# Graph network with LSTM windows on one core: first loads split over two queues, constants awaited later, and the rounding of the recurrent weights moved from VectorE to ScalarE

## What is computed

```
h = relu(adj @ (x @ Wg0 + bg0))
h = relu(adj @ (h @ Wg1 + bg1))
for p in 1..4:                       # windows of p nodes, last hidden state written back
    last = lstm_last(Wih[p-1], Whh[p-1], bih[p-1], bhh[p-1], windows(h, p))
    h[:, idx] = last
x = layernorm(x + h)
agg = A_hat @ x                      # adj + I, scaled by 1/sqrt(degree) on both sides
out = batchnorm(relu(batchnorm(agg @ W1.T + b1)) @ W2.T + b2)
x = layernorm(x + out)
```

## Time and profile before

| | |
|---|---|
| median of 3 runs | 818.66 us (818.16 to 818.75) |
| the profiled execution | 818.31 us, its span 816.5 us |
| PE busy | 782.5 us (96%), 4952 matmuls |
| DVE busy | 719.1 us (88%) |
| ACT busy | 591.8 us (72%) |
| POOL busy | 73.7 us (9%) |
| chain that ended last | PE 79%, DVE 10%, ACT 6% |
| mean granted TensorE clock | 0.992 |

### The profile page before, as it was taken

One profiled execution on the slowest core, in us unless ns is written; L12 is line 12 of the kernel. 1 busy time (PEld: TensorE's weight loads), 2 busy tenths in 40 slices (PEclk: granted clock), 3 DMA queues, 4 the chain that ended last, 5 costly groups with the idle time before them and its releaser, 6 DMA issues.

```text
span 816.5 us, 15519 instructions
## 1 busy us (share of the span) xinstructions
PE 782.5 (96%) x4952; PEld 535.3 (66%) x4952; DVE 719.1 (88%) x1819; ACT 591.8 (72%) x1178; POOL 73.7 (9%) x76
## 2 busy tenths in 40 slices
PE   8999999999999999999999999999999977899985
PEld 5666777777767776777677767776765754344542
DVE  4787989999999999999999999999999986588897
ACT  4666777777777777777777777777777853794398
POOL 0000000000000000000000000000000000000696
PEclk9999999999999999999999999999999999999998
DMA  6010001010101010101010101010000101144245
GB/s 198 26 50 3 1 27 53 34 45 27 52 28 52 26 51 26 51 26 51 26 51 26 51 26 51 27 53 27 26 26 27 53 27 51 53 153 155 77 177 210
DMA packets 17693, 44.97 MB, mean 55 GB/s; under 512 B 2032, under 2 KB 3184, under 8 KB 17520
## 3 DMA queue, kind: packets, MB, share of 16 engines
q1 hardware_dynamic: 17648, 44.39, 15.4%
HBM read 27.61 MB, written 16.78 MB: 54 GB/s over the span
## 4 chain that ended last, share of the span: by engine, by line
PE 79%; DVE 10%; ACT 6%; issue 2%; POOL 1%; DMA 1%; SPq 1%; ACTq 0%; DVEq 0%; POOLq 0%
PE gate_bank L902 14%; PE gate_bank L903 14%; PE gate_bank L939 7%; PE gate_bank L917 6%; PE gate_bank L927 6%; PE back_bank L856 3%; PE front_bank L821 3%; PE front_bank L810 3%; ACT z L1050 3%; PE front_bank L827 3%; PE front_bank L815 3%; PE gate_bank L886 3%; PE gate_bank L887 2%; PE gate_bank L888 2%; PE gate_bank L910 2%
## 5 line engine op out<-in xcount | busy, mean ns | idle before, releaser
L902 PE MATMUL gate_bank<-h_hi,w_hi 128*128 128x256 f16 (+2 forms) x528 | 161.9, 307 | 4.4 <-DVE h_lo L1263 2.9
L903 PE MATMUL gate_bank<-h_hi,w_lo 128*128 128x256 f16 (+2 forms) x528 | 161.7, 306 | 0.0
L1000 ACT ACTIVATE gate_i<-gate_bank,lstm_bias 128x512 f32<-128x512 f32 (+2 forms) x176 | 99.5, 566 | 62.3 <-PE gate_bank L927 32.1
L1000 ACT ACTIVATE gate_o<-gate_bank,lstm_bias 128x512 f32<-128x512 f32 (+2 forms) x176 | 100.0, 568 | 30.4 <-PE gate_bank L927 20.0
L917 PE MATMUL gate_bank<-h_lo,w_hi 128*128 128x256 f16 (+2 forms) x384 | 115.8, 301 | 0.0
L902 PE MATMUL gate_bank<-s_hi,w_hi 128*128 128x256 f16 (+2 forms) x384 | 112.7, 302 | 1.3 <-DVE s_hi L1260 1.3
L903 PE MATMUL gate_bank<-s_hi,w_lo 128*128 128x256 f16 (+2 forms) x384 | 112.6, 302 | 0.0
L1246 DVE SCALAR_TENSOR_TENSOR gate_f<-gate_o,gate_f 128x512 f32<-128x512 f32 (+2 forms) x176 | 94.8, 539 | 19.1 <-ACT gate_f L1006 18.1
L1006 ACT ACTIVATE gate_f<-cell 128x512 f32<-128x512 f32 (+2 forms) x176 | 89.7, 510 | 29.1 <-DVE cell L1243 14.8
L1000 ACT ACTIVATE gate_g<-gate_bank,lstm_bias 128x512 f32<-128x512 f32 (+2 forms) x176 | 99.5, 565 | 0.6
L927 PE MATMUL gate_bank<-s_lo,w_hi 128*128 128x256 f16 (+2 forms) x384 | 99.2, 302 | 0.0
(11 more groups left out here) (195 smaller groups left out, 1665.3 us busy)
## 6 DMA issues: line engine op xcount, KB each, us to landing
x_front<-in_x SPq DMA_DIRECT2D x16, 512.0 KB, 4.1
rows_sb<-in_x SPq DMA_DIRECT2D x16, 512.0 KB, 3.3
x_kept<-normed_sb SPq DMA_DIRECT2D x16, 512.0 KB, 2.6
z<-x_kept SPq DMA_DIRECT2D x16, 512.0 KB, 3.7
out<-z SPq DMA_DIRECT2D x15, 512.0 KB, 3.1
z<-in_wr SPq DMA_DIRECT2D x1, 1536.0 KB, 7.1
out<-z SPq DMA_DIRECT2D x2, 256.0 KB, 2.6
z<-in_wih SPq DMA_DIRECT2D x1, 192.0 KB, 2.6
```

The lines of the kernel that those rows point to most:

```text
L902: mm(dst, w[0], v[0], start=start, stop=False)
L903: mm(dst, w[1], v[0], start=False, stop=False)
L1000: ins = activation(acts[gate][h][:, 0:n], gate_bank[h][bank_of(job, gate)][:, 0:n], ACT.Tanh if gate == "g" else ACT.Sigmoid, bias=lstm_bi ...
```

## The change

Six things are done.

1. adjT_sb is no longer loaded by SP but by ACT, as its first instruction. SP loads x_front of half-step (0, 0) in two parts of 256 KB, and PE waits for the first part in front of mix0's first bank and for the second in front of the second bank.
2. ACT runs a sigmoid of one column first, so that its table load of the sigmoid set comes at the start.
3. DVE's wait for the eight constants, the sum of the LSTM biases and the scaled identity move from in front of lin0's biases to behind them, into split_input_weights.
4. The rounding of slice 0 of w_hi is done by ACT, behind mix1's second output of half-step (0, 0), where ACT now waits for w_stage.
5. The rounding of slices 1 and 2 and of gw1_hi is done by ACT, behind the second relu of lin0 of half-step (0, 1).
6. DVE keeps the subtractions at their old places and waits there for ACT's semaphore weights_high.

```diff
@@ -629,8 +631,8 @@
-            sp.dma_start(adjT_sb[:], adjT).then_inc(sem_adjT, 16)
-            sp.dma_start(flat(x_front[:]), x[0]).then_inc(sem_x, 16)
+            sp.dma_start(x_front[:, 0, :], x[0][:, 0:BANK]).then_inc(sem_x_first, 16)
+            sp.dma_start(x_front[:, 1, :], x[0][:, BANK:2 * BANK]).then_inc(sem_x, 16)
@@ -801,7 +803,10 @@
                 if stage == "mix0":
-                    if (n, i) == (0, 0):
+                    if isinstance(g, int) and (g, h) == (0, 0):
+                        if i == 0:
+                            pe.wait_ge(sem_x if n else sem_x_first, 16)
+                    elif (n, i) == (0, 0):
                         pe.wait_ge(sem_x, loads(g, h))
@@ -982,8 +987,31 @@
             activation = nc.scalar.activation
+            act.dma_start(adjT_sb[:], adjT).then_inc(sem_adjT, 16)
+
+            act.wait_ge(sem_zeros, 1)
+            activation(small[:, 0:1], s_hi[0][:, 0:1], ACT.Sigmoid)
+
+            def weights_high(s):
+                activation(w_hi[:, s], w_stage[:, s], ACT.Copy, scale=W_SCALE).then_inc(sem_high, 1)
+
+            def first_weights():
+                act.wait_ge(sem_wr, 16)
+                weights_high(0)
+
+            def other_weights():
+                weights_high(1)
+                weights_high(2)
+                activation(gw1_hi[:], gw1_stage, ACT.Copy, scale=W_SCALE).then_inc(sem_high, 1)
+
+            first_pair = {(0, ("mix1", "out", 1)): first_weights, (1, ("lin0", "out", 1)): other_weights}
...
@@ -1091,10 +1119,6 @@
             ve.tensor_copy(bias0[:], setup_bank[:, 0:P]).then_inc(sem_degree, 1)
-            dve.wait_ge(sem_loaded, 16 * LOADS)
-            ve.tensor_tensor(lstm_bias[:], lstm_bias[:], bhh_sb[:], ALU.add).then_inc(sem_setup, 1)
-            dve.wait_ge(sem_setup_pool, 1)
-            ve.tensor_scalar(normed_sb[:, 1, P:2 * P], ident[:], small[:, 3:4], None, ALU.mult).then_inc(sem_setup, 1)
             dve.wait_ge(sem_degree, 5)
@@ -1103,16 +1127,19 @@
             def split_input_weights():
 
+                dve.wait_ge(sem_loaded, 16 * LOADS)
                 ve.tensor_copy(wih1_hi[:], wih1_stage).then_inc(sem_wih, 1)
                 dve.wait_ge(sem_wih, 1)
                 ve.tensor_tensor(wih1_lo[:], wih1_stage, wih1_hi[:].bitcast(F32), ALU.subtract).then_inc(sem_wih, 1)
+                ve.tensor_tensor(lstm_bias[:], lstm_bias[:], bhh_sb[:], ALU.add).then_inc(sem_setup, 1)
+                dve.wait_ge(sem_setup_pool, 1)
+                ve.tensor_scalar(normed_sb[:, 1, P:2 * P], ident[:], small[:, 3:4], None, ALU.mult).then_inc(sem_setup, 1)
 
             def split_weights(s):
 
                 if s == 0:
                     dve.wait_ge(sem_wr, 16)
-                ve.tensor_scalar(w_hi[:, s], w_stage[:, s], W_SCALE, None, ALU.mult).then_inc(sem_degree, 1)
-                dve.wait_ge(sem_degree, 6 + s)
+                dve.wait_ge(sem_high, s + 1)
@@ -1120,8 +1147,7 @@
             def prepare_back():
 
-                ve.tensor_scalar(gw1_hi[:], gw1_stage, W_SCALE, None, ALU.mult).then_inc(sem_degree, 1)
-                dve.wait_ge(sem_degree, 9)
+                dve.wait_ge(sem_high, 4)
```

More of the change, by code:

```diff
@@ L518, in gnn_lstm_kernel @@
         sem_x = sem("x_front_loaded")
+        sem_x_first = sem("x_first_loaded")
+        sem_high = sem("weights_high")
         sem_xb = sem("x_back_loaded")
```

4 lines of the change are left out of this document (added).

## The result

The changed kernel took 814.58 us (median of 5 executions, 814.04 to 815.33), the kernel before 818.2 us beside it (5 executions, 816.94 to 818.75): a ratio of 0.9962 with an interval of 0.9948 to 0.9976. A second measurement with more executions gave 815.38 us (9, from 813.87 to 816.74) against 818.33 us (21, from 815.36 to 820.24), a ratio of 0.9968, 0.9957 to 0.9979. The medians lie 3.6 and 3.0 us apart; the ratios make it 3.1 and 2.6 us, and by the intervals anything from 1.7 to 4.3 us.

What follows compares the result with a forecast made beforehand. PE was taken to bound the loop, and VectorE to be what others wait for between 40 and 50 us. Gains of 0.84 + 0.72 + 0.31 = 1.87 us off 818.66 gave 816.8 us, range 815.2 to 818.2.

Steps and rivals of the forecast that it cites:

- The start: Before 16.97 us: gates about 1.4 us earlier, counted as 0 because PE waits for the second x_front; bounds 0 and 1.4.
- Place one: Around 18 to 23 us: VectorE loses a rounding, hidden state up to 0.5 us earlier, 0.12 carried on.
- Place two: 24 to 30 us: VectorE loses a 0.72 us rounding; with 0.12 carried on, PE starts 0.84 us earlier.
- ScalarE's block: Three roundings on ScalarE before h_hi, 24 to 30 us: 2.55 us, costing 0 up to 2.77 us, 0.4 at 3.15.
- Place three: 40 to 48 us: VectorE drops a rounding before `mixed`, gain 0.72 us; bounds 0.3 and 0.72.
- Place four: 50 to 53 us: gw1's rounding leaves VectorE, `h_lo` comes earlier, gain 0.31 us; bounds 0.1 and 0.4.
- The sum: Whole kernel: 0.84 + 0.72 + 0.31 = 1.87 us gained, profiled execution 818.31 to 816.44 us; chance 0.60.
- The clock at the end: Last half-step and tail: no term in the sum; nothing more was to come after 50 to 53 us.
- The median shown: Whole kernel: median 0.35 us above the profiled execution, so 818.66 - 1.87 = 816.8 us.
- More than summed: Rival at the start: second x_front lands earlier or isn't PE's stop, so 1.4 us count too: 815.4 us; chance 0.08.
- Slower, by the clock: Rival: PE's clock falls in its idle time before 16.97 us, 3.3 us lost, 1.87 won: 820.1 us; chance 0.04.

Runs made afterwards that it cites:

- the start alone: Changed kernel with all roundings back on VectorE, keeping its loads, early table load and late constants: 816.63 us, ratio 0.9987.
- the roundings alone: Changed kernel with the old loads, constants' wait, bias sum and scaled identity, keeping roundings and early table load on ScalarE: 814.82 us, ratio 0.9967.
- 28 zero matmuls: 28 instead of 20 matmuls on zeros before the last half-step's and the tail's products: kernel before 815.92 us, changed kernel 813.54 us.
- a variant: Changed kernel with the rounding of slice 2 back on VectorE: 816.13 us, ratio 0.9979.
- the one execution of 1158.64 us: Sixth execution of the changed kernel with 28 instead of 20 matmuls on zeros, mean granted clock 0.653; that run's median was 813.54 us.

## Why the prediction came out too high

- **The start, counted as nothing: right within the landing's scatter, for this order of loads.** It brought lin1 forward by 1.69 us and PE's work on the second x_front by 0.15; averaged over seven profiles with it and four without, by 0.13. The change without its start runs as fast (ratio 0.9967 against 0.9968), and moving that one load forward by one place brings 1.1 us. The reason given, a landing 0.09 us ahead of PE's start, was enough to see it.
- **Place one, 0.12 carried on: too small.** From x_front to the bias at lin0 (22.98 before, 22.56 after) it is 6.01 us before and 5.74 after, so 0.27 was carried; 0.15 more came with the landing. The step that failed here is "its products release the biases from 22.98 on". In the kernel before, lin0's product ran from 21.66 and VectorE was the late one, busy without a gap up to the bias:

```profile
21.66 1.02 PE L815 MATMUL front_bank<-mixed,w_sb 128*128 128x512 f32 x2
...
22.38 0.68 DVE L1237 TENSOR_TENSOR cell<-gate_i,gate_g 128x512 f32<-128x512 f32 x1
```

  The product was there by 22.68 and the bias began at 22.98, 0.60 us behind the start of the cell. With a rounding less, VectorE is ready sooner, and the bias follows the product at once (21.50 + 1.02 = 22.52, bias at 22.56). From x_front to place two it was 12.48 us before, 12.24 with the start alone, 11.40 with the roundings alone (0.72 of the 1.08 is the rounding at place two) and 11.50 with both: either part gives the carry (0.24 and 0.36), and both together give it once (0.26).
- **Place two, 0.84: 1.13 measured.** The rounding is worth 0.72 as summed, 28.32 - 27.58 = 0.74 from `mixed` to PE is as before, and the 0.29 over it are the two items of place one.
- **ScalarE's block: right.** Estimated 1.07 for 128x1024, 0.41 for gw1 and 2.55 for the block; the rows have 1.06, 0.40 and 2.34 (24.77 to 27.11, since two roundings in a row overlap and take 1.99). The reader at 28.18 found h_hi written.
- **Place three, 0.72: 0.90 measured** (18.24 us from place two before, 17.34 after). The rounding itself is worth 0.74: that is the run with it given back (18.08) against the change. The other 0.16 is a step that I had not in the sum. From the split at 43.91 to the bias at 44.41 it is 0.50 us before, and 42.06 to 42.40 = 0.34 after. The product that this bias reads is no part of it, since it began at 41.81 and was done 1.6 us ahead. Before, from VectorE's and PE's timelines:

```profile
43.91 0.43 DVE L1260 CAST h_hi<-gate_f 128x512 f16<-128x512 f32 x1
44.41 0.69 DVE L1160 TENSOR_TENSOR h0T<-back_bank,bias 128x512 f32<-128x512 f32 x1
...
41.81 1.02 PE L815 MATMUL back_bank<-mixed,w_sb 128*128 128x512 f32 x2
```

  and in the run with the rounding of slice 2 back on VectorE:

```profile
44.58 0.43 DVE L1289 CAST h_hi<-gate_f 128x512 f16<-128x512 f32 x1
44.93 0.68 DVE L1189 TENSOR_TENSOR h0T<-back_bank,bias 128x512 f32<-128x512 f32 x1
```

  The step is 0.35 there and 0.50 in the run with the start alone. So it goes with the other roundings that left VectorE and not with the one of place three; why it shrinks is open.
- **Place four, 0.31: 0.32 measured.**
- **The sum: 1.87 forecast, 2.35 to 2.4 in the trace.** The first rstd averages 98.02 us over three profiles (the kernel before twice, and with 28 zero matmuls) and 95.54 over the same three of the changed kernel: 2.5 us. Of these, 0.3 are landings (PE's start on the second x_front averages 16.90 and 16.61), and 2.2 lie behind it.
- **The clock at the end: put at nothing, and this is the largest miss.** The sum takes 1.87 us off the profiled execution (818.31) and then off "The median shown", 0.35 above it, as if all the rest of the time stood still. For the clock, the prediction says "no row of this trace shows it". The trace of the kernel before does show it: PE idles for 2.54 us in front of 686.28, and the products behind took 1.77 + 1.92 us, with a granted clock of 0.50 from 687 us on. In that profile the two stretches at the end have their long forms (13.59 and 61.44 us), which other executions of the same kernel have shorter, by 1.3 and 1.7 us, and the range had no term for it.
- **The miss added up.** The profiled execution of the changed kernel is also its median, 814.58 us, 2.2 below the 816.8 forecast: 0.5 from the places that were sized too small and the landing, 1.3 from the clock at the last half-step, and 0.35 from the step from the profiled execution to the median. The first is the change's but for the landing; the other two are luck of the draw. That the clock's places also shift the medians is argued from the profiles and the granted clocks, as only one execution of each run is profiled. On the second measurement the forecast's ratio of 816.8 / 818.66 = 0.9977 is just inside the interval.
- **The rivals.** "More than summed" had the nearest time (815.4) by a mechanism that didn't occur. "Slower, by the clock" did occur, in one profile of a variant, for 1.57 us. That execution took 818.21 us, so nothing of the gain was left in it (the kernel before had a median of 817.6 beside it), while the median of its run stayed a gain. The Trainium skill, "TensorE: Matmul & The Clock Gate", on oscillation, says that PE's idle gaps, there waits for a DMA, throttle the engine again. The rows behind 1.81 us of idle time in that one profile agree (0.50), and so do those behind 2.54 us near 686 us in the kernel before; those behind 1.85 us in the kernel before and 1.52 us in the changed kernel don't. The rule on multiplications of the Trainium skill's "ScalarE: Activation LUTs", in its rules for kernel authors, would have left the roundings with VectorE. The rows agree that ScalarE is the slower one (1.06 us against 0.69), but giving back the one rounding of place three cost 0.74 us.

Left open: whether the changed kernel draws the falls of the clock at the end as often as the kernel before (too few profiles to say); what decides in which execution the clock falls near 17, 658, 678, 686 or 700 us, and the one execution of 1158.64 us.

## What to carry to other kernels

An operation is worth moving to a slower engine when the trace shows the faster one as the releaser of the waits, and the slower one idle in front of the place: here 0.69 us off VectorE cost ScalarE 1.06, and nobody waited. Before a start is made shorter, look for the next load that everything stands behind, and for what goes ahead of it in its queue: the shorter start by itself gave 0.2 us in the trace, and 1.1 more once the load was one place earlier. And before a gain of 0.3% is believed or sized from two profiles, compare them stretch by stretch and take a second profile of the same kernel, since only what comes back in every execution can be put down to the change.

## What the runs showed of the hardware

- TensorE's clock falls in some executions of a kernel and not in others, at the same instructions. With PE idle 2.54 us behind 20 matmuls on zeros, the two groups of products behind took 1.77 + 1.92 us instead of 1.16 + 1.16, and the stretch grew by 1.3 us; when the fall came while the zeros ran (6.17 us for 20 instead of 4.48), the stretch had its short form. Where the fall lands matters: a fall between 656 and 664 us made the loop 0.6 us longer (585.87 for 585.30), and one of 7 us there 2.0 us.
- A load issued 0.47 us earlier and ahead of 512 KB landed 1.1 us earlier (7.81 + 7.9 = 15.71 for 8.28 + 8.5 = 16.78). In the changed kernel's profile the loads move some 360 to 450 GB/s in this part, so 512 KB are about 1.3 us (an estimate). With nothing changed, the same load took from 8.1 to 8.7 us from issue to landing.
- ScalarE wrote 128x1024 float16 from float32 in 1.06 us, VectorE in 0.69. Two of them in a row took 1.99, so they overlap by 0.13.
- The table load moved to the start costs 1.28 us there, unseen, as the engine had nothing else to do.
